# Starting the stacking copies of queries and keys as each bf16 part is written

## What is computed

```python
def _L1_attn_ref(x, qkv_w, qkv_b, qkv_B, proj_w, proj_b, proj_B):
    ...
    qkv = x @ qkv_w.T + qkv_b
    qkv = qkv.reshape(B, N, 3, NUM_HEADS, hd).transpose(2, 0, 3, 1, 4)
    q, k, v = (qkv[0], qkv[1], qkv[2])
    attn = jnp.einsum('bhnd,bhmd->bhnm', q, k) * scale
    attn = jax.nn.softmax(attn, axis=-1)
    out = jnp.einsum('bhnm,bhmd->bhnd', attn, v)
```

## Time and profile before

| | us |
|---|---|
| median of 3 runs | 4890.29 |
| lowest and highest | 4887.49 to 4894.54 |
| profiled execution, its own time | 4889.78 |
| profiled execution, span of its instructions | 4888.1 |

### The profile page before, as it was taken

How to read it: one execution, slowest core, us unless ns; L and a number is a source line. 1 busy time by engine, 2 the same in 40 slices (tenths; PEclk the granted TensorE clock), 3 DMA queues, 4 the chain that set the end, 5 groups by cost and what they waited for, 6 DMA issues and landing times.

```text
span 4888.1 us, 70094 instructions
## 1 busy us (share of the span) xinstructions
PE 4106.4 (84%) x27744; PEld 3173.8 (65%) x27744; DVE 2643.1 (54%) x7217; ACT 1747.0 (36%) x2774; POOL 398.9 (8%) x523
## 2 busy tenths in 40 slices
PE   2678888888888888888888888888888888888888
PEld 1556666666666666666666666666666666666666
DVE  2346555555555555555555555555555555556443
ACT  1223333433333333333334333333333343333332
POOL 2100000000000000000000000000000000000000
PEclk8668898888889988899888889888889899889888
DMA  4011111011111111111101111101111101111000
GB/s 112 23 29 34 26 35 29 27 30 32 26 35 32 30 25 30 29 32 32 32 24 30 35 26 32 32 24 29 36 26 32 32 24 33 32 26 19 13 13 4
DMA packets 154046, 147.13 MB, mean 30 GB/s; under 512 B 64359, under 2 KB 132026, under 8 KB 153722
## 3 DMA queue, kind: packets, MB, share of 16 engines
q1 hardware_dynamic: 153722, 142.64, 13.4%
HBM read 87.28 MB, written 7.91 MB: 19 GB/s over the span
## 4 chain that ended last, share of the span: by engine, by line
PE 58%; DVE 19%; SPq 5%; POOL 5%; ACT 5%; issue 5%; DMA 4%; DVEq 0%; POOLq 0%; ACTq 0%
PE area_n L1031 12%; PE area_m L1031 9%; PE area_a L1023 9%; PE area_b L1023 5%; SPq L451 5%; PE area_n L1248 4%; DMA k1s<-scratch 3%; DVE xn L730 3%; DVE mx L927 2%; PE area_n L1055 2%; PE area_a L1106 2%; PE area_m L1198 2%; ACT pT_both L655 2%; DVE part L744 2%; PE area_a L1031 1%
## 5 line engine op out<-in xcount | busy, mean ns | idle before, releaser
L927 DVE TENSOR_REDUCE mx<-area_n 91x1 f32<-91x273 f32 x1152 | 467.0, 432 | 361.1 <-PE area_n L1248 356.5
L1031 PE MATMUL area_n<-w_dn,hid 128*91 128x192 f32 x2304 | 476.4, 370 | 68.9 <-DVE mrow L932 33.5
L1023 PE MATMUL area_a<-xT,w_gu 96*128 96x273 f32 x1536 | 442.5, 435 | 68.9 <-ACT pa L600 52.4
L1031 PEld LDWEIGHTS area_n<-w_dn,hid 128*91 128x91 f32 x2304 | 411.6, 184 | 117.4 <-issue 87.2
L1248 PE MATMUL area_n<-k1s,q1s 96*91 96x273 bf16 x1152 | 349.1, 353 | 146.8 <-DMA k1s<-scratch 98.5
L1023 PEld LDWEIGHTS area_a<-xT,w_gu 96*128 96x128 f32 x1536 | 312.3, 211 | 175.8 <-ACT pa L600 62.7
L1023 PE MATMUL area_b<-xT,w_gu 96*128 96x273 f32 x1536 | 387.8, 395 | 0.0
L600 ACT ACTIVATE pa<-area_a,scal 91x820 bf16<-91x820 f32 x192 | 180.0, 938 | 544.1 <-PE area_a L1106 492.1
L1248 PEld LDWEIGHTS area_n<-k1s,q1s 96*91 96x91 bf16 x1152 | 144.4, 139 | 287.7 <-DVE mx L927 131.3
L1023 PEld LDWEIGHTS area_b<-xT,w_gu 96*128 96x128 f32 x1536 | 287.8, 191 | 59.7 <-issue 0.3
L990 DVE SCALAR_TENSOR_TENSOR outb<-area_n,cwt,outb 91x192 f32<-91x192 f32 x288 | 102.0, 407 | 396.0 <-PE area_n L1031 396.0
(11 more groups left out here) (242 smaller groups left out, 7550.3 us busy)
## 6 DMA issues: line engine op xcount, KB each, us to landing
img<-in_x SPq DMA_DIRECT2D x192, 392.0 KB, 3.5
q1s<-scratch SPq DMA_DIRECT2D x192, 102.4 KB, 3.5
k1s<-scratch SPq DMA_DIRECT2D x192, 102.4 KB, 4.3
out<-outb SPq DMA_DIRECT2D x32, 204.8 KB
q0s<-scratch SPq DMA_DIRECT2D x128, 25.6 KB, 3.3
k0s<-scratch SPq DMA_DIRECT2D x128, 25.6 KB, 2.0
pooled<-pooled_dram SPq DMA_DIRECT2D x128, 9.2 KB
tokens<-in_txt SPq DMA_DIRECT2D x32, 57.8 KB
```

Source lines behind the costliest of these rows:

```text
L927: v.tensor_reduce(mx[:, k:k + 1], N[0:TC, k % 2, 0:T], AX.X, ALU.max)\
L1023: last = mm(area[x][0:rows_, j, 0:n], w(j, kc), rhs[:, kc, 0:n], start=(kc == 0), stop=(kc == NK - 1))
L1031: last = mm(by_token(x)[:, c, :], lhs(i, c), w_, start=(i == 0), stop=(i == len(w) - 1))
```

## The change

SP no longer waits once for all three parts. For the queries and then for the keys it waits for part 0 (ACT's `taken`), issues the three copies that read it, waits for part 1 (`mids_ready`), issues two, waits for part 2 (`lows_ready`), and issues the last one. The rows of the stack that a copy fills are the same, their order of issue is another. On DVE the rounding to part 1 raises `mids_ready` in place of the shared step counter, and DVE waits for that before it goes on, as it waited for the counter.

```diff
+PARTS_OF = Q_PARTS, K_PARTS
...
-        x32_ready, parts_ready = sem("x32_ready"), sem("parts_ready")
+        x32_ready, mids_ready, lows_ready = sem("x32_ready"), sem("mids_ready"), sem("lows_ready")
...
-                        sp.wait_ge(parts_ready, n * 2 + (k + 1))
-                        for r, p_ in enumerate((Q_PARTS, K_PARTS)[k]):
-                            sp.dma_start((q1s, k1s)[k][HD * r:HD * r + HD, :, :],
-                                         parts[:, k, p_, :, :]).then_inc(stack_in, 16)
+                        for p_ in range(3):
+                            if p_:
+                                sp.wait_ge((mids_ready, lows_ready)[p_ - 1], n * 2 + (k + 1))
+                            else:
+                                t.await_taken(pair_of(name, k), stage)
+                            for r in [r for r, of in enumerate(PARTS_OF[k]) if of == p_]:
+                                sp.dma_start((q1s, k1s)[k][HD * r:HD * r + HD, :, :],
+                                             parts[:, k, p_, :, :]).then_inc(stack_in, 16)
...
-                        link(v.tensor_copy(parts[:, k, 1, :, :], x32[:, k, :, :]))
+                        v.tensor_copy(parts[:, k, 1, :, :], x32[:, k, :, :]).then_inc(mids_ready, 1)
+                        dve.wait_ge(mids_ready, n * 2 + (k + 1))
                         v.tensor_tensor(parts[:, k, 2, :, :], x32[:, k, :, :], parts[:, k, 1, :, :], ALU.subtract)\
-                            .then_inc(parts_ready, 1)
+                            .then_inc(lows_ready, 1)
```

## The result

The kernel with the change takes 4870.51 us (median of 6 runs, 4869.63 to 4877.08); the kernel before took 4892.41 in the same comparison (6 runs, 4887.49 to 4898.83). The ratio is 0.996, with a 95% interval of 0.9948 to 0.9972: a gain of some 22 us, clear of noise, but a sixth of the 125 that were forecast. The forecast of 4765 and its range of 4725 to 4835 both miss. In the runs further down, one execution of e6 (13107.76 us) and one of e7 (5343.88 us, the profiled one, with a clock of 0.732) lie far outside the others; their medians count them and their ratios do not, and e6's ratio leaves out its 4900.10 as well.

What follows compares the result with a forecast made beforehand. It took SP's queue of query and key copies, which PE waits for before `mx.0`, as the path. 4889.8 - 84 (wait) - 41 (clock) = 4764.8, given as 4765 us, range 4725 to 4835.

Steps and rivals of the forecast that it cites:

- The copies: SP's query and key copies before `mx.0`: starting part by part, the last lands 2.0 to 3.3 us sooner a turn.
- The gain of 3.1 us a turn: Last key copy before `mx.0`: lands 3.1 us sooner in each turn, taken from 2.0 to 3.3.
- the 84 us of the forecast: PE's wait before `mx.0`, 98.5 us in all: 84 us of it go, 77 in 29 turns and 7 at the ends.
- the slack of 0.6 us between 3.1 and 2.5: Before `mx.0`: copies come 3.1 us sooner, but PE can use only the 2.52 us it waited.
- PE's next limit: At `mx.0`: once the copies are early, `ey.1`, PE's own work, is late next, so PE is bound by itself.
- The clock term: PE's granted clock behind `mx.0`: fewer long low stretches of 2.9 us each, gaining 0 to 49 us, taken as 41.
- with the wait gone only the stretch after `v1` can bring the clock down: Behind `mx.0`: PE works without a gap before it, so only the little work after `v1` can lower the clock.
- the 41 us: Behind `mx.0`: 14 of 17 long low-clock stretches go, at 2.9 us each, giving 41 us.
- 3 of 17 long stretches: Clock over the turn: 14 of 17 counted, because low stretches elsewhere fall otherwise and some turns may lose.
- The prediction's own sign of being wrong, a mean clock that falls: PE's granted clock: the forecast is wrong if its mean, about 0.87, falls.
- the wait goes, the clock stays as it is: Behind `mx.0`: low stretches as often or traded for others elsewhere; 4806 us, 4826 with smaller copy gain; chance 0.22.
- the slower rival: Rest of the turn: shorter turns meet clock changes elsewhere; two added long low stretches a turn give 4980 us; chance 0.04.

Runs made afterwards that it cites:

- e6: The change plus 20 small extra products (results unused) on PE before `mx.0` in every turn; 4886.93 us, ratio 0.9964 to the kernel before.
- e7: The change plus 40 small extra products (results unused) on PE before `mx.0` in every turn; 4800.59 us, ratio 0.9806 to the kernel before.
- e1: Half of the change: queries' copies begin part by part, keys' only when all three parts are written; 4861.40 us, ratio 0.9931 to the kernel before.
- e13: The kernel before with its one wait, but the six copies issued in the change's order (part 0 three times, part 1 twice, part 2); 4947.98 us, ratio 1.0120.
- e3: The change plus small extra products (results unused) at five places where PE waits for other engines; 4826.12 us, ratio 0.9863 to the kernel before.
- e4: The kernel before, without the change, plus small extra products (results unused) at five places where PE waits; 4910.48 us, ratio 1.0037.
- e10: The kernel before, without the change, plus 80 extra products (2.4 us) in PE's idle time before `mx.0`; 4891.45 us, ratio 0.9993.
- e2: Other half of the change: keys' copies begin part by part, queries' only when all three parts are written; 4943.59 us, ratio 1.0110 to the kernel before.
- e8: The change plus 80 extra products (2.4 us a turn) on PE before `mx.0`; 4823.68 us, ratio 0.9860 to the kernel before.
- e14: The change plus 90 extra products (2.7 us a turn) on PE before `mx.0`; 4912.66 us, ratio 1.0043 to the kernel before.
- e9: The change plus 40 extra products before `mx.0`, the same kernel as e7 measured again; 4810.22 us, ratio 0.9825 to the kernel before.
- e11: The change plus 40 extra products before `a2.6`, late in the turn, instead of before `mx.0`; 4852.23 us, ratio 0.9907 to the kernel before.
- e12: The change plus 55 extra products (1.65 us a turn) on PE before `mx.0`; 4867.54 us, ratio 0.9943 to the kernel before.

## Why the prediction was wrong

**The copies: right.** The gain of 3.1 us a turn could not be read from `mx.0` any more, since PE is the later one now, but the wait fell from 98.5 to 15.4 us. That is the 84 us of the forecast (83.1), and nearly all of it comes from the queries (e1). The added waits of SP and the traded one of DVE cost nothing that the traces show. What the working missed is the order of the copies: it holds the last landing back by 0.37 us a turn (e13), for which the slack of 0.6 us between 3.1 and 2.5 leaves room.

**PE's next limit: right, nearly.** `mx.0` starts behind `ey.1` without a gap, and no wait of that length came in its place. Two things show it: PE's idle time fell by 70.2 us (781.7 to 711.5, span less busy time), and the filled pair e3 and e4 stands the whole wait apart. The 13 us between 83.1 and 70.2 are small waits that grew; the largest is PE's for ACT's `selT`, 10.9 us before and 20.9 after, 0.3 us a turn.

**The clock term: wrong, in sign and size.** The failing step is the sentence that "with the wait gone only the stretch after `v1` can bring the clock down", with "at least nothing" as the bound below it, and the 41 us that were built on both. The long low stretch behind `mx.0` did go with the wait: 0.57 over the first 12 us in 17 turns before and in none after, and in none of e10, where the wait is filled and not removed. But other parts of the turn can bring the clock down too. The clock now falls 18 to 30 us behind `mx.0`, in every turn of the middle, where it stood at 0.97 or more, and PE has dense work there. For this trade the working had set aside 3 of 17 long stretches, 9 us. The low clock with a product running costs 68 us more, not 41 less. That is 109 us of the 112 by which the profiled execution missed the forecast (4876.8 - 4764.8); the copies' term is 1 off, and 2 are left. The prediction's own sign of being wrong, a mean clock that falls, is there: 0.871 to 0.858.

The Trainium skill's page "TensorE: Matmul & The Clock Gate" says in "A second HAM failure mode: psum-queue depth-cycling" that short idles let the clock swing. The traces agree so far, as the clock swings several times in a turn, and with the idle time before `mx.0` filled (e10) the swing behind it is shorter. It doesn't follow that one idle less leaves the mean higher: here it went from 0.871 to 0.858.

The account of wait and clock can be drawn up for every kernel. Without extra products, the span, less the wait for the key copies and less the low clock's cost with a product running, leaves 4269 us before, 4272 for the change, 4268 in e1, 4272 in e2 and 4271 in e13. Five kernels whose spans cover 79 us agree within some 4 once the two are taken off; with (1 - clock) x span in place of the second they agree within 11 (4159 to 4170). For the kernels with products before `mx.0`, less their work at 0.0325 us each, the first account leaves 4264 to 4279, though their spans cover 112 us. With (1 - clock) x span it would be 4146 to 4193, so there the mean clock alone is too coarse a measure.

**The rivals.** The one that came true is "the wait goes, the clock stays as it is" in its mechanism, but worse, and not quite: it allowed for low stretches "traded for others elsewhere in the turn", at no net cost. The mechanism of the slower rival, a shorter turn that meets the clock's changes at other points, is what took most of the gain. I gave it 0.04 and priced it only as all or nothing, two long stretches in every turn. What I never drew from it is the middle: one stretch more in part of the turns. The 17 long turns of 28 were the warning. They said that turns of equal work differ by 2.9 us by the clock alone, and could have told me that one stretch more or less in every turn is 28 x 2.9 = 81 us. The term that I bounded by 0 and 49 us, as a gain, should have been bounded by -81 and +81, and the range should have reached to 4887.

**What stays open.** That the place of the work in the turn matters, and not its amount alone, is shown (e8 against e14, e9 against e11). By what rule the clock picks its stretches, and so which amount of work is a good one, was not found; neither e12 nor e14 was foretold. Nor is it shown why turns settle on these lengths.

**A faster version.** The change with 40 idle products (e7, e9) beats both kernels: 4800.59 and 4810.22 us, measured twice, 1.8 to 1.9% under the kernel before. It is a setting found by trial that holds for this program as it stands; e12's 15 products more lose most of it, and one execution with 40 took 5343.88 us.

## What to carry to other kernels

Where PE's granted clock changes several times in every pass of a loop, a wait that is removed from the chain is worth its length plus or minus what the new position of the work does to the clock, and the second term can be as large as the first. Look for it in the kernel before: passes with equal work and unequal length, told apart by the clock alone, give the size of that term, and it belongs in the range on both sides. After such a change compare the low clock's cost beside the waits, counting only the low time in which PE works, and try small shifts of the work before judging the change by one time.

## What the runs showed of the hardware

- Work added to PE can make a kernel faster: 1.2 us of useless products a turn took it from 4871 to 4801 and 4810 us, with a clock of 0.882 instead of 0.858.
- The turns of the loop settle on a few exact lengths: 143.36 us in e8, 146.77 in e14 and e6, 143.97 and 146.16 by turns in the kernel after, 144.00 and 146.13 in e12. 0.3 us more of work a turn moved nearly all of them from 143.36 to 146.77 (e8 and e14).
- The same mean clock can cost quite different amounts: 0.876 and 0.873 in e8 and e14, with PE busy for 4141.4 and 4205.8 us, of which 10 are added work.
- With the idle time before `mx.0` filled with products, the clock over the next 12 us is 0.86 in 26 of 28 turns instead of 0.57 in 17 of them, and lower elsewhere in the turn; the time of the kernel stays (e10).
- Twelve copies of the same bytes from the same buffer land 0.37 us later when those that read the same part are issued next to each other and part 2 last (wait of 110.4 against 98.5 us over 32 turns).
- In the five traces in which PE waits for the key copies in the middle turns (before, e2, e4, e10, e13) the turns scatter; in the ten others, e7's aside, they repeat after the first turns, singly or in short cycles (e1 with some breaks). That the scatter of the landings keeps them from settling is a reading of this, not shown by itself.
